# A router's tie count joined with its comparison, a choice made between two rankings, and the end of six tiles shared out over ScalarE and GpSimd

## The chip, the core and the metric

The kernel runs on one core of a Trainium2 chip. The metric is the device time of one execution in microseconds (us). Five engines work at once, each through its own queue in program order: TensorE (PE), VectorE (DVE), ScalarE (ACT), GpSimd (POOL) and SyncE (SP), which here only issues transfers. They wait for each other on counting semaphores.

## The reference, cut to what matters

All is float32. Two attention layers come first, then a mixture of experts, and at last a block that only the best three quarters of each batch's tokens go through:

```python
x = x + attention_2(attention_1(x, ...), ...)        # (2, 1024, 256)
h = moe(x)            # 8 experts, best 2 per token, plus one shared expert
x = x + ffn(h)

def moe(x):           # T = 2048 tokens
    scores = softmax((x @ wt.T + repeat(g @ wg.T)) / 2)
    w, idx = top_k(scores, 2);  w = w / (w.sum(-1) + 1e-20)
    y_e  = (leaky(x @ w_gate[e]) * (x @ w_up[e])) @ w_down[e]
    p    = (leaky(x @ sw_gate) * (x @ sw_up)) @ sw_down
    return sum over the two chosen e of w * y_e, + p

def ffn(h):           # (B, L, D) = (2, 1024, 256)
    k = int(L * 0.75)                                # 768 of 1024 tokens of a batch
    scores = einsum('bld,d->bl', h, w_router)
    _, top_idx = top_k(scores, k)
    processed = gelu(h[b, top_idx] @ w_block)
    return h.at[b, top_idx].set(processed)           # the others stay as they are
```

A token's score is higher than another's, or equal and at a lower index: that is the order that `top_k` uses, so equal scores have to be counted apart.

## The kernel before

The change lies in the last stage, some 60 us of 386, and in its preparation. P is 128, N is 1024 tokens to a batch, B is 2, TB is 8 tiles of 128 tokens to a batch, NT is 16 tiles in all, and NC_ is 4 chunks c of TT = 4 tiles, so that batch 0 is chunks 0 and 1 and batch 1 is chunks 2 and 3. Everything is written out by hand, with one program for each engine, and every engine keeps to its order.

**Sum of the experts.** The routed experts' results lie in the DRAM array YS, two rows to a token. SyncE reads them by chunks into YR (line 2327, 1 MB each, two buffers). Chunks 2 and 3 are read when VectorE is through with chunks 0 and 1. VectorE adds both rows, weighted, to the shared expert's result in Y (line 2748): for each chunk four tiles with k = 0, then four with k = 1, counted in `s_y`.

**Scores.** For each chunk TensorE turns Y (`result_turned`, line 2534), ScalarE copies it to FT (line 2617, two copies), TensorE makes the scores (`scores`, line 2542), ScalarE copies them to SR (line 2619), and TensorE lays each token's own score in a column (`own_scores`, line 2549). The four chunks follow each other, with the turning of chunk c + 1 ahead of `own_scores(c)`.

**Products.** `through_block(c)` (line 2557) multiplies a chunk's four tiles by w_block, two PSUM buffers in turn, and ScalarE applies the gelu (line 2623) to GE. All 16 tiles come behind the scores of all chunks, on TensorE as on ScalarE: `through_block(0)`, `masks_counted(0)`, `through_block(1)` to `(3)`, `masks_counted(1)`.

**Ranking.** `compare(b)` on VectorE goes through the 8 tiles q of a batch. Line 2761 compares the scores of tiles q to 7 with the tile's own scores, writes the mask GT[q] in bf16 and sums it into cnt. Line 2764 then counts the equal scores of lower index within the tile, into the scratch eqj. `masks_counted(b)` on TensorE (line 2573) adds up the masks of the tiles before (28 small products), so that what is counted in one direction need not be compared in the other. `compare(1)` writes over the same GT, and so waits for `masks_counted(0)`. `choose(b)` (lines 2772 to 2776) makes the rank, and `sel`, which is 1 for a token that goes through the block.

**End.** GpSimd makes Z = X1 + Y (line 2392), then GE = GE - Y (line 2395), each for all 16 tiles. VectorE makes Z = Z + sel * GE for all 16 (`finish`, line 2782; the profile names Z as WGU, GE as X, and X1 as AI, whose memory they use). SyncE writes the four chunks out in order (line 2331, 512 KB each). The order on VectorE is:

```python
compare(0)
compare(1)
choose(0)
finish(0)
choose(1)
finish(1)
```

## Time and profile before

| | us |
|---|---|
| median of 3 runs | 388.48 |
| lowest and highest | 386.22, 388.92 |
| profiled execution, its own time | 387.94 |
| its span, first to last instruction | 386.2 |
| TensorE busy in the span | 306.6 (79%) |
| VectorE busy | 207.0 (54%) |
| GpSimd busy | 182.3 (47%) |
| ScalarE busy | 135.9 (35%) |
| mean granted TensorE clock | 0.900 |

The busy shares are averages over all stages. The last stage begins at 330.48 us, when SyncE issues the first read of YS, so the questions about it are answered by the chain of waits and the timeline from there on. In what follows a time of day such as 364.93 is counted from the start of the span. A merged line of the timeline, such as "x8", gives the start of its first instruction and the time to the end of its last.

### The profile page before, as it was taken

To read this page: it belongs to the slowest core of one execution; us is meant where nothing else is said; L and a number is where in the kernel's file an instruction comes from. 1 tells how busy PE (TensorE), PEld (TensorE's weight loads), DVE (VectorE), ACT (ScalarE), POOL (GpSimd) and SP (SyncE) were. 2 spreads that over 40 slices of the span, in tenths; PEclk is the share of its full clock that TensorE was granted. 3 is DMA by queue.
4 is the path that set the end of the run, shared out by engine and by line. 5 is a ranking of instruction groups with operands and counts; after the bars stand their busy time and mean duration, and the time that the engine had idled before them with its cause. 6 is when DMAs were issued, how large, how long until landed. Compare 5 with 4: busy or idle time off the path is not lost.

```text
span 386.2 us, 5777 instructions
## 1 busy us (share of the span) xinstructions
PE 306.6 (79%) x1625; PEld 209.6 (54%) x1625; DVE 207.0 (54%) x730; ACT 135.9 (35%) x428; POOL 182.3 (47%) x306
## 2 busy tenths in 40 slices
PE   0499999988998978977692999719999997068990
PEld 0246767655774735443531665418888885035680
DVE  0724555521742237796458344504555553199996
ACT  1146676753111166572210000003555554014440
POOL 1308998863020000167404878732666666166380
PEclk9999999999999685798896799968999999558996
DMA  4779950000019800000100222243555441642006
GB/s 129 218 188 276 309 151 3 2 0 1 2 48 299 186 0 0 3 0 0 29 1 35 88 98 82 92 125 98 161 158 165 146 126 43 207 133 98 0 2 218
DMA packets 36186, 37.84 MB, mean 98 GB/s; under 512 B 5423, under 2 KB 31792, under 8 KB 36147
## 3 DMA queue, kind: packets, MB, share of 16 engines
q1 hardware_dynamic: 31762, 28.90, 26.5%
q0 software_dynamic: 3408, 8.41, 6.2%
q8 instruction: 17, 0.28, 0.3%
q10 hardware_dynamic: 976, 0.08, 0.2%
q14 instruction: 23, 0.18, 0.2%
HBM read 21.74 MB, written 16.55 MB: 99 GB/s over the span
## 4 chain that ended last, share of the span: by engine, by line
PE 22%; POOL 11%; DVE 9%; DMA 5%; issue 4%; ACT 1%; DVEq 0%; POOLq 0%; SPq 0%
PE psU L2489 9%; POOL XS L2369 4%; PE psY L2507 4%; POOL XS L2378 4%; DVE Y L2748 3%; DMA YR<-YS 3%; PE psG L2479 2%; POOL pause L2358 2%; DVE WGU L2782 2%; DVE GT L2761 2%; PE psY L2499 1%; PE psU L2557 1%; PE psG L2413 1%; PE psU L2413 1%; DVE eqj L2764 1%
## 5 line engine op out<-in xcount | busy, mean ns | idle before, releaser
L2386 POOL DMA_INDIRECT YS<-YB,IB x39 | 38.4, 984 | 36.3 <-issue 23.6
L2489 PE MATMUL psU<-WGU,XT 128*128 x156 | 42.1, 394 | 0.1
L2599 ACT COPY XT<-psG 128x256 f32<-128x256 f32 x39 | 14.7, 377 | 64.5 <-PE psG L2479 64.5
L1195 POOL TENSOR_SCALAR UU<-UU,rs 128x257 f32<-128x257 f32 x32 | 29.8, 931 | 0.0
L2489 PEld LDWEIGHTS psU<-WGU,XT 128*128 128x128 f32 x156 | 27.7, 198 | 2.8 <-issue 0.5
L1360 ACT ACTIVATE UU<-UU,nm 128x129 f32<-128x129 f32 x64 | 28.4, 453 | 0.7 <-DVE nm L1469 0.7
L1469 DVE CUSTOM_DVE_ANT_0 UU<-psS,BI 128x129 f32<-128x129 f32 x64 | 19.1, 356 | 17.2 <-PE psS L1248 17.2
L1194 POOL TENSOR_SCALAR UU<-UU,rs 128x129 f32<-128x129 f32 x32 | 19.6, 612 | 16.6 <-DVE rs L1479 16.4
L2369 POOL DMA_INDIRECT XS<-AI,SI x16 | 15.7, 981 | 23.1 <-DVE SI L2688 18.9
L2732 DVE TENSOR_SCALAR LK<-psU 128x128 f32<-128x128 f32 x39 | 11.4, 292 | 26.6 <-PE psU L2489 26.1
L2748 DVE SCALAR_TENSOR_TENSOR Y<-YR,W,Y 128x256 f32<-128x256 f32 x32 | 18.2, 640 | 12.5 <-DMA YR<-YS 12.5
L857 POOL TENSOR_TENSOR T<-Vn,wn 128x128 f32<-128x128 f32 x8 | 3.0, 401 | 46.4 <-DVE wn L953 46.3
L2424 PE MATMUL psY<-SD,HH 128*128 128x256 f32 x64 | 17.1, 415 | 7.9 <-DVE HH L2714 7.9
L2507 PE MATMUL psY<-WD,HT 128*128 x78 | 23.3, 382 | 0.0
L2479 PE MATMUL psG<-ident,XB 128*128 128x128 f32 x78 | 15.5, 285 | 9.4 <-DMA XB<-XS 9.4
L2424 PEld LDWEIGHTS psY<-SD,HH 128*128 128x128 f32 x64 | 13.1, 207 | 12.8 <-issue 10.3
L2392 POOL TENSOR_TENSOR WGU<-AI,Y 128x256 f32<-128x256 f32 x16 | 13.0, 840 | 14.4 <-DVE Y L2748 14.4
L1487 DVE COPY PT<-psTt 128x384 f32<-128x384 f32 x16 | 8.9, 555 | 20.3 <-PE psTt L1319 20.3
L930 DVE CUSTOM_DVE_ANT_0 UU<-psS,RA,NL 128x256 f32<-128x256 f32 x32 | 13.7, 480 | 10.4 <-ACT RA L797 9.6
L2479 PEld LDWEIGHTS psG<-ident,XB 128*128 128x128 f32 x78 | 11.4, 148 | 13.8 <-issue 10.2
L2606 ACT COPY HT<-psY 128x128 f32<-128x128 f32 x39 | 10.3, 265 | 22.3 <-PE psY L2499 21.7
L2534 PE MATMUL psG<-ident,Y 128*128 128x128 f32 x32 | 6.0, 349 | 14.9 <-DVE Y L2748 14.9
(313 smaller groups left out, 740.8 us busy)
## 6 DMA issues: line engine op xcount, KB each, us to landing
XS<-PZ SPq DMA_DIRECT2D x1, 5011.5 KB, 21.2
XB<-XS SPq DMA_DIRECT2D x39, 128.5 KB
YR<-YS SPq DMA_DIRECT2D x4, 1024.0 KB, 5.5
BI<-in_bias SPq DMA_DIRECT2D x4, 512.0 KB, 8.8
out_dram<-WGU SPq DMA_DIRECT2D x4, 512.0 KB, 3.0
X<-in_x SPq DMA_DIRECT2D x2, 768.0 KB, 9.8
BI<-in_bias SPq DMA_DIRECT2D x4, 256.0 KB, 8.0
Wo<-in_wo SPq DMA_DIRECT2D x1, 1024.0 KB, 6.9
```

The costliest lines, as they stand in the source:

```text
L1194: pool.tensor_scalar(U[:, he, 0:W1], U[:, he, 0:W1], rs[:, d, 2 * he:2 * he + 1], None, ALU.mult)
L1195: pool.tensor_scalar(U[:, he, W1:WU], U[:, he, W1:WU], rs[:, d, 2 * he + 1:2 * he + 2], None, ALU.mult).then_inc(n_done, 1)
L1360: act.activation(U[:, he, cols], U[:, he, cols], ACT.Exp, scale=-1.0, bias=nm[:, d, n:n + 1], accum_out=rs[:, d, n:n + 1]).then_inc(exp_do ...
L1469: dve.tensor_tensor_reduce(out=U[:, he, cols], in0=psS[2 * (d % 2) + he][:, cols], in1=BI[:, h, cols], scale=-1.0, scalar=-NEG, op0=ALU.ad ...
L2369: pool.indirect_dma_start(XS[:, :], bass.IndirectOffsetOnAxis(ap=SI[:, 0, t:t + 1], axis=0), AI[:, t, :], None).then_inc(s_g0[t // TB], 16)
L2378: pool.indirect_dma_start(XS[:, :], bass.IndirectOffsetOnAxis(ap=SI[:, 1, t:t + 1], axis=0), AI[:, t, :], None).then_inc(s_g1, 16)
L2386: pool.indirect_dma_start(YS[:, :], bass.IndirectOffsetOnAxis(ap=IB[:, b, n:n + 1], axis=0), YB[i][:, n, :], None, bounds_check=2 * NTOK - ...
L2424: mm = pe.matmul(psY[c % 2][:, t, :], HH[n % 2][:, t * P:(t + 1) * P], SD[:, m, :], start=m == 0 and t % 2 == 0, stop=m == NS_ - 1, skip_g ...
L2479: mm = pe.transpose(psG[b % 2][:, (k * SUB + n) * P:(k * SUB + n + 1) * P], XB[b % RING][:, n, k * P:(k + 1) * P], ident[:, :])
L2489: mm = pe.matmul(psU[b % 2][:, n * D:(n + 1) * D], XT[b % 2][:, k, n * P:(n + 1) * P], WGU[:, k, bass.ds(which[b], 1), :].rearrange("p a m ...
L2507: mm = pe.matmul(result(b)[:, n * D:(n + 1) * D], HT[b % 2][:, n * P:(n + 1) * P], WD[:, bass.ds(which[b], 1), :].rearrange("p a d -> p (a ...
L2748: dve.scalar_tensor_tensor(out=Y[:, t, :], in0=YR[c % 2][:, t % TT, k, :], scalar=W2[:, k, t:t + 1], in1=Y[:, t, :], op0=ALU.mult, op1=ALU ...
```

## The change

- In `compare`, the whole-row comparison starts one tile later and is left out for q = 7. The tile on the diagonal is compared by the other instruction, which takes `is_gt` in place of `is_equal`, multiplies by `upper` in place of `low`, and writes the first 128 columns of GT[q]. eqj is gone. TensorE now adds the diagonal masks too: 36 small products in place of 28.
- The sums that this leaves over are put into `need`, before the shared expert, with one reduction and one subtraction more on VectorE.
- `choose(0)` moves from behind `compare(1)` to within it, ahead of its first mask.
- `through_block(0)` moves from behind the scores of all chunks to behind `own_scores(1)`, and its four gelus move to behind chunk 1's copy to SR on ScalarE.
- Tiles 2 to 7 are ended without VectorE: ScalarE multiplies GE by `sel` (a copy with a scale, placed behind the gelu of tile u + 8) and GpSimd adds it to Z (placed behind the subtraction of tile u + 8). VectorE ends tiles 0, 1 and 8 to 15.
- The first read of YS becomes two, of two tiles each. VectorE starts on the first two tiles at the first of them.
- The chunks are written out in the order 0, 2, 1, 3. Chunks 0 and 1 wait for GpSimd's count as well as VectorE's.

```diff
@@ -2211,9 +2211,9 @@
                 low = tensor(st, "low", [P, P])
                 one_b = tensor(st, "one_b", [P, 1], BF16)
                 GT = [[tensor(st, f"GT{i}{q}", [P, (TB - q) * P], BF16) for q in range(TB)] for i in range(1)][0]
-                eqj = tensor(st, "eqj", [P, 4, P])
                 cnt = tensor(st, "cnt", [P, NT, 2])
                 need = tensor(st, "need", [P, TB])
+                ahead = tensor(st, "ahead", [P, 1])
                 rank = tensor(st, "rank", [P, NT])
                 sel = tensor(st, "sel", [P, NT])
                 GE = X
@@ -2232,7 +2232,7 @@
                 s_pe = sem(st, "s_pe")
                 PE_GUIDED, PE_LOGITS, PE_TURNED, PE_TOTAL, PE_PLACES = 1, 2, 3, 4, 5
                 s_route = sem(st, "s_route")
-                GUIDES, READ, SHIFTED, MARKED, TOTALS, SLOTTED, SLOT_IDS, EXPERT_IDS = range(1, 9)
+                GUIDES, READ, SHIFTED, MARKED, TOTALS, SLOTTED, SLOT_IDS, EXPERT_IDS, CHOSEN = range(1, 10)
                 s_ex = sem(st, "s_ex")
                 s_g0 = [sem(st, f"s_g0{g}") for g in range(2)]
                 s_i1 = sem(st, "s_i1")
@@ -2270,6 +2270,11 @@
                 blk = st.enter_context(nc.Block())
 
                 SPACED = 2 * NT - 1
+                DIFFERENT = SPACED + NT + TB
+                BY_DVE = 2
+                ENDED = [0]
+                for u in range(TB):
+                    ENDED.append(ENDED[-1] + (2 if u >= BY_DVE else 1))
 
                 def bank(c, k):
 
@@ -2321,13 +2326,18 @@
                     for i in range(RING):
                         sp.wait_ge(s_ys[i], 16 * SUB * len(range(i, NBK, RING)))
                     picks = YS.rearrange("(t p k) d -> p t k d", p=P, k=2)
+                    sp.dma_start(YR[0][:, 0:2, :, :], picks[:, 0:2, :, :]).then_inc(s_xb[0], 16)
                     for c in range(NC_):
                         if c >= 2:
                             sp.wait_ge(s_y, 2 * TT * (c - 1))
-                        sp.dma_start(YR[c % 2][:, :, :, :], picks[:, TT * c:TT * c + TT, :, :]).then_inc(s_yr[c % 2], 16)
+                        lo = 0 if c else 2
+                        sp.dma_start(YR[c % 2][:, lo:TT, :, :], picks[:, TT * c + lo:TT * c + TT, :, :]
+                                     ).then_inc(s_yr[c % 2], 16)
                     ov = out.rearrange("b (t p) d -> p (b t) d", p=P)
-                    for c in range(NC_):
-                        sp.wait_ge(s_z, TT * c + TT)
+                    for c in (0, 2, 1, 3):
+                        if c < 2:
+                            sp.wait_ge(pool_done, DIFFERENT + ENDED[TT * c + TT])
+                        sp.wait_ge(s_z, (BY_DVE, BY_DVE, BY_DVE + TT, BY_DVE + 2 * TT)[c])
                         sp.dma_start(ov[:, TT * c:TT * c + TT, :], Z[:, TT * c:TT * c + TT, :]).then_inc(s_out, 16)
                     sp.wait_ge(s_out, 16 * NC_)
 
@@ -2390,9 +2400,18 @@
                     for t in range(NT):
                         pool.wait_ge(s_y, 2 * TT * (t // TT) + TT + t % TT + 1)
                         pool.tensor_tensor(Z[:, t, :], X1[:, t, :], Y[:, t, :], ALU.add).then_inc(pool_done, 1)
-                    for t in range(NT):
+                    for t in range(TB):
                         pool.wait_ge(s_ge, t + 1)
                         pool.tensor_tensor(GE[:, t, :], GE[:, t, :], Y[:, t, :], ALU.subtract).then_inc(pool_done, 1)
+                    pool.wait_ge(pool_done, DIFFERENT)
+                    pool.wait_ge(s_route, CHOSEN)
+                    for t in range(TB, NT):
+                        pool.wait_ge(s_ge, t + 1)
+                        pool.tensor_tensor(GE[:, t, :], GE[:, t, :], Y[:, t, :], ALU.subtract).then_inc(pool_done, 1)
+                        u = t - TB
+                        if u >= BY_DVE:
+                            pool.wait_ge(s_ex, 2 + u - BY_DVE)
+                            pool.tensor_tensor(Z[:, u, :], Z[:, u, :], GE[:, u, :], ALU.add).then_inc(pool_done, 1)
 
                 @blk.tensor
                 def _(pe):
@@ -2565,16 +2584,18 @@
                         if c + 1 < NC_:
                             result_turned(c + 1)
                         own_scores(c)
+                        if c == 1:
+                            through_block(0)
+
                     def masks_counted(b):
-                        for q in range(1, TB):
+                        for q in range(TB):
                             t = b * TB + q
-                            pe.wait_ge(s_gt, t)
-                            for a in range(q):
+                            pe.wait_ge(s_gt, t + 1)
+                            for a in range(q + 1):
                                 mm = pe.matmul(larger(t), GT[a][:, (q - a) * P:(q - a + 1) * P], one_b[:, :],
-                                               start=a == 0, stop=a == q - 1)
+                                               start=a == 0, stop=a == q)
                             mm.then_inc(s_cs, 1)
 
-                    through_block(0)
                     masks_counted(0)
                     for c in range(1, NC_):
                         through_block(c)
@@ -2618,9 +2639,14 @@
                         act.wait_ge(s_sc, c + 1)
                         act.copy(SR[:, :, :].rearrange("p b n -> p (b n)")[:, c * CH:(c + 1) * CH], scored(c)
                                  ).then_inc(s_sr, 1)
-                    for t in range(NT):
-                        act.wait_ge(s_h, t + 1)
-                        act.activation(GE[:, t, :], psU[t % 2][:, 0:D], ACT.Gelu_apprx_tanh).then_inc(s_ge, 1)
+                        for t in (range(TT) if c == 1 else range(TT, NT) if c == NC_ - 1 else ()):
+                            act.wait_ge(s_h, t + 1)
+                            act.activation(GE[:, t, :], psU[t % 2][:, 0:D], ACT.Gelu_apprx_tanh).then_inc(s_ge, 1)
+                            u = t - TB
+                            if u >= BY_DVE:
+                                act.wait_ge(s_route, CHOSEN)
+                                act.wait_ge(pool_done, DIFFERENT)
+                                act.activation(GE[:, u, :], GE[:, u, :], ACT.Copy, scale=sel[:, u:u + 1]).then_inc(s_ex, 1)
 
                 @blk.vector
                 def _(dve):
@@ -2701,7 +2727,10 @@
                     dve.wait_ge(s_wb, 32)
                     for k in range(KD):
                         dve.tensor_copy(wr_m[:, k, :], wr_c[:, k:k + 1].broadcast_to([P, P])).then_inc(s_wr, 1)
-                    chain(dve.tensor_scalar(need[:, :], exp_f[:, 0:TB], -float(P), float(TOPK), ALU.mult, ALU.add))
+                    dve.wait_ge(s_con, 10)
+                    chain(dve.tensor_reduce(ahead[:, :], low[:, :], AX_X, ALU.add), True)
+                    chain(dve.tensor_scalar(need[:, :], exp_f[:, 0:TB], -float(P), float(TOPK), ALU.mult, ALU.add), True)
+                    chain(dve.tensor_tensor(need[:, :], need[:, :], ahead[:, 0:1].broadcast_to([P, TB]), ALU.subtract), True)
                     chain(dve.memset(cnt[:, :, :], 0.0), True)
 
                     for n in range(NJ + 1):
@@ -2740,9 +2769,14 @@
                     dve.wait_ge(bh_done, NBK)
                     for c in range(NC_):
                         tiles = range(TT * c, TT * c + TT)
-                        dve.wait_ge(s_yr[c % 2], 16 * (c // 2 + 1))
+                        if c:
+                            dve.wait_ge(s_yr[c % 2], 16 * (c // 2 + 1))
+                        else:
+                            dve.wait_ge(s_xb[0], 16 * (len(range(0, NBK, RING)) + 1))
                         for k in range(2):
                             for t in tiles:
+                                if not c and not k and t == 2:
+                                    dve.wait_ge(s_yr[0], 16)
                                 if k:
                                     dve.wait_ge(s_y, 2 * TT * c + t % TT + 1)
                                 dve.scalar_tensor_tensor(out=Y[:, t, :], in0=YR[c % 2][:, t % TT, k, :], scalar=W2[:, k, t:t + 1],
@@ -2754,40 +2788,41 @@
                         ts = slice(b * TB, b * TB + TB)
                         chain(dve.tensor_copy(SC[:, ts], bank(3, b)[:, 0:TB]), True)
                         if b:
-                            dve.wait_ge(s_cs, b * (TB - 1))
+                            choose(0)
                         for q in range(TB):
                             t = b * TB + q
                             own = SC[:, t:t + 1]
-                            dve.tensor_scalar(GT[q][:, :], SR[:, b, q * P:N], own, 0.0, ALU.is_gt, ALU.add,
-                                              accum_out=cnt[:, t, 0:1]).then_inc(s_gt, 1)
-                            after(3)
-                            chain(dve.scalar_tensor_tensor(out=eqj[:, count[0] % 4, :], in0=SR[:, b, q * P:(q + 1) * P],
-                                                           scalar=own, in1=low[:, :], op0=ALU.is_equal, op1=ALU.mult,
-                                                           accum_out=cnt[:, t, 1:2]))
+                            if q + 1 < TB:
+                                chain(dve.tensor_scalar(GT[q][:, P:], SR[:, b, (q + 1) * P:N], own, 0.0, ALU.is_gt, ALU.add,
+                                                        accum_out=cnt[:, t, 0:1]))
+                            dve.scalar_tensor_tensor(out=GT[q][:, 0:P], in0=SR[:, b, q * P:(q + 1) * P], scalar=own,
+                                                     in1=upper[:, :], op0=ALU.is_gt, op1=ALU.mult,
+                                                     accum_out=cnt[:, t, 1:2]).then_inc(s_gt, 1)
 
                     def choose(b):
                         ts = slice(b * TB, b * TB + TB)
                         dve.wait_ge(s_gt, TB * (b + 1))
                         after()
                         chain(dve.tensor_reduce(rank[:, ts], cnt[:, ts, :], AX_X, ALU.add), True)
-                        dve.wait_ge(s_cs, (b + 1) * (TB - 1))
-                        chain(dve.tensor_tensor(rank[:, b * TB + 1:b * TB + TB], rank[:, b * TB + 1:b * TB + TB],
-                                                psG[b][:, 1:TB], ALU.subtract), True)
-                        chain(dve.tensor_tensor(sel[:, ts], rank[:, ts], need[:, :], ALU.is_lt), True)
-
-                    def finish(b):
-                        dve.wait_ge(pool_done, SPACED + b * TB + TB)
-                        for t in range(b * TB, b * TB + TB):
-                            dve.wait_ge(pool_done, SPACED + NT + t + 1)
-                            dve.scalar_tensor_tensor(out=Z[:, t, :], in0=GE[:, t, :], scalar=sel[:, t:t + 1],
-                                                     in1=Z[:, t, :], op0=ALU.mult, op1=ALU.add).then_inc(s_z, 1)
+                        dve.wait_ge(s_cs, (b + 1) * TB)
+                        chain(dve.tensor_tensor(rank[:, b * TB:b * TB + TB], rank[:, b * TB:b * TB + TB],
+                                                psG[b][:, 0:TB], ALU.subtract), True)
+                        dve.tensor_tensor(sel[:, ts], rank[:, ts], need[:, :], ALU.is_lt).then_inc(s_route, 1)
+                        dve.wait_ge(s_route, CHOSEN + b)
+
+                    def finish(t):
+                        dve.scalar_tensor_tensor(out=Z[:, t, :], in0=GE[:, t, :], scalar=sel[:, t:t + 1],
+                                                 in1=Z[:, t, :], op0=ALU.mult, op1=ALU.add).then_inc(s_z, 1)
 
                     compare(0)
                     compare(1)
-                    choose(0)
-                    finish(0)
+                    dve.wait_ge(pool_done, DIFFERENT)
+                    for t in range(BY_DVE):
+                        finish(t)
                     choose(1)
-                    finish(1)
+                    for t in range(TB, NT):
+                        dve.wait_ge(pool_done, DIFFERENT + ENDED[t - TB] + 1)
+                        finish(t)
 
 
 
```

## Rows read from the trace of the kernel before

**Rows 1.** Page, its first line.
```profile
span 386.2 us, 5777 instructions
```
**Rows 2.** Chain that ended last, in order of time, last stage: start us, us, what.
```profile
330.48 5.52 DMA YR<-YS
...
345.54 5.39 DMA YR<-YS
...
360.48 3.65 PE psU L2557 x16
```
**Rows 3.** Timeline, ScalarE and TensorE: start us, us, engine, line, op, idle before.
```profile
352.08 1.08 ACT L2617 COPY FT<-psG 128x512 f32<-128x512 f32 x2
352.36 0.40 PE L2549 MATMUL psY<-ident,SR 1*128 1x1 f32 x4
353.21 1.98 PE L2542 MATMUL psY<-FT,wr_m 128*128 128x512 f32 x4 [0.45 <-ACT FT L2617]
355.60 1.09 PE L2534 MATMUL psG<-ident,Y 128*128 128x128 f32 x8 [0.40 <-DVE Y L2748]
...
359.44 0.58 ACT L2619 COPY SR<-psY 128x512 f32<-128x512 f32 x1 [2.07 <-PE psY L2542]
360.04 1.28 ACT L2623 ACT_TABLE_LOAD   x1
...
361.58 0.38 ACT L2623 ACTIVATE X<-psU 128x256 f32<-128x256 f32 x1 [0.26 <-PE psU L2557]
...
364.17 0.38 ACT L2623 ACTIVATE X<-psU 128x256 f32<-128x256 f32 x1 [0.48 <-PE psU L2557]
...
364.67 10.61 PE L2557 MATMUL psU<-WB,FT 128*128 128x256 f32 x48
...
375.12 0.84 PE L2573 MATMUL psG<-one_b,GT 128*128 128x1 bf16 x28
```
**Rows 4.** Timeline, VectorE: two steps of compare(0), then compare(1) begins.
```profile
355.65 1.28 DVE L2761 TENSOR_SCALAR_CACHE_REDUCE GT<-SR,SC 128x1024 bf16<-128x1024 f32 x1
...
356.86 0.35 DVE L2764 SCALAR_TENSOR_TENSOR eqj<-SR,SC,low 128x128 f32<-128x128 f32 x1
...
357.13 1.14 DVE L2761 TENSOR_SCALAR_CACHE_REDUCE GT<-SR,SC 128x896 bf16<-128x896 f32 x1
...
364.93 1.28 DVE L2761 TENSOR_SCALAR_CACHE_REDUCE GT<-SR,SC 128x1024 bf16<-128x1024 f32 x1 [0.21 <-PE psG L2573]
```
**Rows 5.** Timeline, the end: choice, last eight of finish, and the four writes.
```profile
374.38 0.16 DVE L2774 TENSOR_TENSOR rank<-rank,psG 128x7 f32<-128x7 f32 x1
...
374.83 4.20 DVE L2782 SCALAR_TENSOR_TENSOR WGU<-X,sel,WGU 128x256 f32<-128x256 f32 x8
...
377.48 5.73 SPq L2331 DMA_DIRECT2D out_dram<-WGU  x4
...
379.55 3.26 DVE L2782 SCALAR_TENSOR_TENSOR WGU<-X,sel,WGU 128x256 f32<-128x256 f32 x8
...
381.25 0.37 SPq L2331 DMA_DIRECT2D out_dram<-WGU  x1
```
**Rows 6.** Timelines, GpSimd beside VectorE, then GpSimd alone.
```profile
339.46 2.46 POOL L2392 TENSOR_TENSOR WGU<-AI,Y 128x256 f32<-128x256 f32 x3
...
339.70 1.72 DVE L2748 SCALAR_TENSOR_TENSOR Y<-YR,W,Y 128x256 f32<-128x256 f32 x2
...
177.73 2.10 POOL L871 TENSOR_TENSOR AI<-X,CB 128x256 f32<-128x256 f32 x3
```
**Rows 7.** Windows, after TensorE's last work: busy by engine, clock, DMA share, GB/s.
```profile
380.20:380.40 0.20, 0.00 (x0) 0.00 (x0) 0.20 (x2) 0.00 (x0) 0.00 (x0) 0.83 1.00 343
```
**Rows 8.** Groups by line: TensorE's wait ahead of the routed experts, then ScalarE's forms.
```profile
L2479 PE MATMUL psG<-ident,XB 128*128 128x128 f32 x78 | 15.5, 285 | 9.4 <-DMA XB<-XS 9.4
...
L813 ACT ACTIVATE UU<-UU,nm 128x256 f32<-128x256 f32 x32 | 15.8, 499 | 0.0
L2623 ACT ACT_TABLE_LOAD x1 | 1.3, 1283 | 0.0
```

## Prediction

> **What bounds the kernel now.** I read the chain of waits first. From 330.48 us on it tells of one serial stretch: the read of YS, the sums over chunks 0 and 1, from 345.54 the read of chunk 3, and VectorE's last sums, until its comparisons begin at 355.65 [rows 2, 4]. The busy shares would have said TensorE, but in this stage the bound changes hands, so I went through the timeline piece by piece.
>
> First, TensorE and ScalarE carry chunks 2 and 3 to the scores, and both wait for each other: products 1.98, copy 0.58, and so on [rows 3]. `own_scores(3)` ends about 360.48, `through_block(0)` takes 3.65 more [rows 2], and `masks_counted(0)` follows. Second, VectorE starts compare(0) at 355.65 and compare(1) at 364.93 [rows 4], and is never idle for long until the end. TensorE has by then 12 tiles of products to do, from 364.67 for 10.61 us, and `masks_counted(1)` ends at 375.96 (375.12 + 0.84) [rows 3]. So the two run nearly level, TensorE to 375.96 and VectorE's comparisons to about 374.1. Third, VectorE alone does the sixteen steps of finish, from 374.83 to 382.81 (379.55 + 3.26) [rows 5]. The last write is issued at 382.84 (377.48 + 5.73, less the 0.37 of one issue), and the span ends at 386.2 [rows 1, 5]: 3.35 us behind a single last write.
>
> **The reads of YS.** VectorE starts on half of chunk 0 at the first transfer. The second half still has to come, and by the chain the whole 1 MB lands 5.52 us after its issue [rows 2]. So only the two steps that can be done ahead are won. One step takes 0.40 us: (3.26 - 0.48)/7 in the last finish, of the same form [rows 5]. That is 0.8 us at most. The second issue costs SyncE 0.37 of it at worst, so I take 0.6, between 0.4 and 0.8. Chunks 2 and 3 wait in the same chain and move up with it. VectorE's comparisons then begin at 355.05, and `own_scores(1)` ends at 352.16 (352.36 + 0.40 - 0.6) [rows 3].
>
> **Through_block(0) moved up.** It costs TensorE 3.65 us again, 352.16 to 355.81. But ScalarE keeps its order, and FT of chunk 2 now stands behind four gelus. The load of the gelu's table, 1.28 us, starts when the copy to SR is done, about 351.5, and ends about 352.8; the first gelu comes 1.10 after the start of the products (360.48 to 361.58), so at 353.3, and the load is hidden [rows 2, 3]. The fourth gelu ended 0.42 after the four tiles' products (364.17 + 0.38 against 360.48 + 3.65), so now at 356.23. Then come two copies to FT, 1.08 [rows 3], so `scores(2)` starts at 357.38; before it started at 353.21. From there on nothing waits for VectorE any more. The steps are: scores 1.98, turning and the two copies behind the copy to SR 1.77, scores 2.0, copy and wait 0.66, own scores 0.41. Sum 6.8: `own_scores(3)` ends at 364.2. Before, the same point came at 360.48, but with 3.65 of products still to do, that is at 364.13. **So what is moved up gains nothing.** The 0.41 us for which TensorE waited for VectorE's sums, and 0.6 of the reads, are paid out again for gelus and copies that once lay beside products and now hold TensorE up for 1.57 us.
>
> How the load's own cost is counted matters here. The trace has 1.28 us of load at 360.04 and the gelu at 361.58, which waited for TensorE by the profile, so at most 0.26 lie behind the load [rows 3]. The Trainium skill (ScalarE: Activation LUTs, What ACT_TABLE_LOAD costs) puts a drain of about 1.38 us beside each load. If it lay behind the load, an estimate from that page would hold chunk 2 back by some 0.5 us more. The row doesn't show it, and the measurement decides.
>
> **Masks and choice.** 36 small products for 28: at 0.84/28 each that is 0.24 more on TensorE, so it ends `masks_counted(0)` at about 365.1. compare(0) lasted at most 9.1 us (355.65 to 364.93, less the wait) and lasts 1.2 less now (below), so it is done at 363 at the latest, and VectorE stands idle for 2 us or more, where before it never waited over 0.21 [rows 4]. It can't go on, because GT is in use, and SR of batch 1 is only there at 363.7. choose(0)'s two last steps, 0.45 (374.38 to 374.83 [rows 5]), now stand ahead of compare(1), which starts at 365.65, against 364.93.
>
> **Compare.** The first step, of 1024 columns, took 1.21 us of VectorE (355.65 to 356.86), and the step on the diagonal 0.27 (356.86 to 357.13) [rows 4]. Each whole-row step becomes one tile shorter and the longest falls away, while the diagonal ones stay: 1.2 us less per batch. The new form of the diagonal step (another comparison, a bf16 result) is in no row. It is nearest to the old one of the same shape, so I take 0.27; it can't come below the 0.13 by which one tile more or less changes a whole-row step (1.28 - 1.14), and at the whole-row step's full price of 0.34 or so it would add 0.5 in a batch. compare(1) lasted 9.2 us (364.93 to about 374.1, just ahead of the choice [rows 4, 5]), so now 8.0: it ends at 373.6, 0.5 earlier. That is all that remains of 2.4 us saved.
>
> **What TensorE still has to do.** 12 tiles from 365.1. In the trace the way from 364.67 to the end of the masks took 11.3 us [rows 3]; with 8 more masks 11.5, so 376.6. VectorE fills the time with finish of tiles 0 and 1, and then waits. sel of batch 1 is there at 377.1, against 379.5 before [rows 5]. The eight last steps of finish would need 3.26 us alone [rows 5], and end at 380.4, 2.4 earlier than now.
>
> **ScalarE's share.** For tiles 10 to 15 a gelu of 0.38 and a copy with a scale stand behind each other. No row has that copy. The lower bound is the gelu's 0.38, the upper 0.50, the exponential from and to SBUF of the same shape [rows 8]. With waits that is 0.8 to 0.93, against 0.863 of one tile on TensorE ((364.17 - 361.58)/3) [rows 3]. I take 0.86, level with TensorE; the upper bound would add 0.4 in six tiles.
>
> **GpSimd's share.** It gets six additions more, and its second eight subtractions wait for choose(0) and for gelu 8, which ends about 370.1. Fourteen steps then follow. Alone, one takes 0.69 us ((2.10 - 0.72)/2). Beside VectorE's steps of two inputs it is different: both go in step, one each in 0.86 (two of VectorE's in 1.72, three of GpSimd's in 2.46), though VectorE alone needs 0.40 [rows 5, 6]. VectorE is at such steps for part of the time, so I take the mean of both: GpSimd ends at 370.1 + 14 x 0.78 = 381.1, and by the bounds 379.8 (0.69) to 382.1 (0.86). VectorE meanwhile makes its four first steps of batch 1 at 0.86, not 0.40. Tiles 8 to 11 are done at 377.15 + 4 x 0.86 = 380.6, tile 15 at about 382.5, against 382.8 before. The saving on VectorE is lost by the contention.
>
> By the Trainium skill (SBUF - State Buffer, SBUF: two separate sides) one of the two engines holds the shared ports for a whole instruction and the other fully blocks. Taken so, a pair would take 0.40 + 0.69 = 1.09, and that is a rival below. The row has 0.86.
>
> **The writes.** A write of 512 KB occupies the queues for 1.53 us at 343 GB/s [rows 7], and the last, alone, needs 3.35 from its issue to the end (above). Chunk 2 is issued at 380.65. Chunk 1 waits for GpSimd's last step, 381.1, and chunk 3 for 382.5. Before, they were spread out. Now three stand within 1.9 us and share the same queues: 380.65 + 3.35 + 2 x 1.53 = 387.1 for the end.
>
> **The sum.** 387.1 against 386.2 of span [rows 1]: 0.9 us longer. What lies around the span, 1.7 us, stays, so 387.94 becomes 388.8. The median of the runs is 0.5 above the profiled execution and they differ by 2.7 among themselves, so I say 388.9. The small work that is added ahead of the shared expert (a reduction, a subtraction, a wait for constants) costs nothing: the shared expert is done so early that TensorE then waits 9.4 us for the routed experts' first transfer [rows 8]. Without that cover it would be some 0.5, at the price of the choice's steps.
>
> **Rivals.** *The forecast: the moved products gain nothing, contention and piled-up writes take the rest*, 387.8 to 389.8, 0.60.
> *The ends don't collide.* If VectorE went on at 0.40 beside GpSimd at 0.69, chunk 2 would be issued at 378.8, chunk 1 at 380.4 and chunk 3 at 380.8: span 385.4, 387.1 in all. The rows of lockstep speak against it, but there GpSimd partly waited for VectorE's result, so it isn't excluded: 0.20.
> *The whole instruction blocks.* At 1.09 per pair tile 11 is done at 381.5, 0.9 later, and the writes with it; with the sums' own delays 389.7 to 390.6. 0.08.
> *ScalarE or TensorE goes slow: the side of over 1% slower.* Each change between gelu and scaled copy could reload the table: 1.28 x 2 for six tiles, 15 us, over 400. It decides from two loads per tile. Against it: one load of 1.28 in the stage, at the first gelu [rows 3], and none for the copies behind an exponential. Or TensorE's clock falls to 1.2 GHz during its new idle time. In the trace it fell at about 380.3, 4.3 us after its last work [rows 3, 7]; the new gaps are 1.6. If it fell, 12 tiles would take 10 us more: 399. Together, and with dearer diagonal steps, 0.07.
> *Faster by over 1%.* The products would have to hide wholly, as if ScalarE could take FT of chunk 2 first: 3.65 less on TensorE, of which compare(0)'s end near 363 lets 2 to 3 through. Even then the span is 384, 2 to 3 less than before, so this needs another gain: 0.05.
>
> **How the numbers follow.** The predicted time is that of the first case. From 386.2 (the second, with 0.9 for the scatter of the runs) to 390.8 (the third) about nine in ten are held with the uncertainty of a median of few runs, so I give 386.2 to 390.8. One per cent is 3.9 us, about what a measurement can tell from no change. Faster by over 1%: 0.05. Slower: 0.07. Within: 0.88.
>
> **What would show it.** `scores(2)` at about 357.4, behind gelu 3 on ScalarE. VectorE idle from about 363 to 365.2, ended by `masks_counted(0)`. compare(1) 1.2 us shorter. `masks_counted(1)` at about 376.6. Steps of finish at 0.86 while GpSimd works. The last three writes within 2 us of each other. The forecast is wrong if ScalarE's copies to FT of chunk 2 don't wait for gelus, if finish goes at 0.40, or if more than one table is loaded in the stage.

## Result, and the profile after

| | before | after |
|---|---|---|
| median, us | 388.43 (20 runs) | 390.74 (20 runs) |
| lowest and highest | 385.38, 392.27 | 387.50, 394.48 |
| ratio after/before, 95% interval | | 1.0069, 1.0043 to 1.0095 |
| profiled execution | 387.94 | 387.5 |
| its span | 386.2 | 385.4 |
| outside its span | 1.74 | 2.10 |

The time moved by 0.7%, so the kernel stayed within 1%, a little slower. The ratios leave out executions over 1.5% above the fastest of their kernel, and by medians the step is 2.3 us (0.6%). The medians mislead a little: ten runs of after lie at 387.5 to 389.6 and ten at 391.9 to 394.5, so that its median falls between two levels, where no run is, while of before 13 lie at 385.4 to 388.9 and seven at 390.9 to 392.3. The means of all twenty are 388.8 and 390.6, 1.8 us apart. The trace says something else: its span is 0.8 us shorter. Two further comparisons (below) gave 0.9988 (0.9950 to 1.0026) and 1.0035 (0.9997 to 1.0073). Most of what follows is about why one trace, one ratio and a sum can disagree by a few us.

The chain of waits of after, last stage (start us, us, what), answers [rows 2]:

```profile
330.90 4.64 DMA YR<-YS
335.54 0.02 issue
335.57 3.40 DVE Y L2782 x6
...
350.24 3.67 PE psU L2576 x16
353.93 0.39 ACT X L2644
354.31 0.97 ACT FT L2638 x2
...
355.33 2.00 PE psY L2561 x4
...
362.03 0.98 PE psG L2595 x36
363.01 10.47 PE psU L2576 x48
373.48 0.89 PE psG L2595 x36
...
375.18 3.50 DVE WGU L2814 x4
```

VectorE's long comparison is gone from the chain; TensorE and ScalarE carry it from 339.11 on. The moved products stand in it at 350.24, and behind them the fourth gelu and the copies to FT of chunk 2, which once lay beside other work.

The timeline of after (start us, us, engine, line, operation, idle before) answers [rows 3] and [rows 5]:

```profile
334.33 0.88 DVE L2782 SCALAR_TENSOR_TENSOR Y<-YR,W,Y 128x256 f32<-128x256 f32 x2 [9.53 <-DMA YR<-YS]
335.57 8.26 DVE L2782 SCALAR_TENSOR_TENSOR Y<-YR,W,Y 128x256 f32<-128x256 f32 x14 [0.35 <-DMA YR<-YS]
...
349.67 1.28 ACT L2644 ACT_TABLE_LOAD   x1
351.33 0.38 ACT L2644 ACTIVATE X<-psU 128x256 f32<-128x256 f32 x1 [0.38 <-PE psU L2576]
...
355.33 1.98 PE L2561 MATMUL psY<-FT,wr_m 128*128 128x512 f32 x4 [1.44 <-ACT FT L2638]
...
362.88 10.61 PE L2576 MATMUL psU<-WB,FT 128*128 128x256 f32 x48
363.12 0.16 DVE L2808 TENSOR_TENSOR rank<-rank,psG 128x8 f32<-128x8 f32 x1 [0.59 <-PE psG L2595]
...
373.93 7.22 SPq L2341 DMA_DIRECT2D out_dram<-WGU  x4
375.18 5.56 DVE L2814 SCALAR_TENSOR_TENSOR WGU<-X,sel,WGU 128x256 f32<-128x256 f32 x8
378.37 0.91 POOL L2414 TENSOR_TENSOR WGU<-WGU,X 128x256 f32<-128x256 f32 x1
```

The last eight steps of finish take 5.56 us, where they took 3.26 [rows 5]: GpSimd works beside the first four, which take 3.50. The last write is issued at 380.78 (373.93 + 7.22 - 0.37), 2.1 earlier than before, but the span ends 4.6 us behind it, not 3.35.

### The profile page after: what moved, and what is told of

Its sections match the earlier page's. It is cut to its first block, busy times and chain, and to the rows that moved or that the text cites. A ratio compares the mean times of both kernels' runs of the same rounds, so it can differ in the third digit from the quotient of the medians.

```text
span 385.4 us, 5821 instructions
## 1 busy us (share of the span) xinstructions
PE 306.7 (80%) x1641; PEld 210.6 (55%) x1641; DVE 205.4 (53%) x722; ACT 138.0 (36%) x434; POOL 186.8 (48%) x312
## 4 chain that ended last, share of the span: by engine, by line
PE 28%; POOL 11%; issue 4%; DVE 3%; DMA 3%; ACT 2%; DVEq 0%; SPq 0%; POOLq 0%
PE psU L2508 9%; POOL XS L2379 4%; PE psY L2526 4%; POOL XS L2388 4%; PE psU L2576 4%; PE psY L2561 3%; PE psG L2498 2%; POOL pause L2368 2%; DVE WGU L2814 1%; DMA YR<-YS 1%; PE psY L2518 1%; ACT FT L2638 1%; PE psG L2432 1%; PE psU L2432 1%; DVE Y L2782 1%
## 5 line engine op out<-in xcount | busy, mean ns | idle before, releaser
L2508 PE MATMUL psU<-WGU,XT 128*128 x156 | 41.3, 389 | 0.1
L2379 POOL DMA_INDIRECT XS<-AI,SI x16 | 15.7, 981 | 24.5 <-DVE SI L2714 20.4
L2388 POOL DMA_INDIRECT XS<-AI,SI x16 | 15.5, 970 | 4.4 <-issue 2.5
```

Of the source, the lines that this page charges most:

```text
L2379: pool.indirect_dma_start(XS[:, :], bass.IndirectOffsetOnAxis(ap=SI[:, 0, t:t + 1], axis=0), AI[:, t, :], None).then_inc(s_g0[t // TB], 16)
L2388: pool.indirect_dma_start(XS[:, :], bass.IndirectOffsetOnAxis(ap=SI[:, 1, t:t + 1], axis=0), AI[:, t, :], None).then_inc(s_g1, 16)
L2508: mm = pe.matmul(psU[b % 2][:, n * D:(n + 1) * D], XT[b % 2][:, k, n * P:(n + 1) * P], WGU[:, k, bass.ds(which[b], 1), :].rearrange("p a m ...
```

## Experiments

Every trace is measured by its last stage, from the first issue of a read of YS to the end of the span, because the start of that stage differs between executions of one and the same kernel. "Total" adds what lies outside the span. "48 products" is the time of the products behind `masks_counted(0)`; its normal value is 10.61. The last three kernels have 40 products there, so the column is empty. Each row is one trace, so a few tenths of a us between two rows can be chance.

| kernel | stage starts | stage | outside | total | 48 products |
|---|---|---|---|---|---|
| before | 330.48 | 55.7 | 1.74 | 57.5 | 10.61 |
| before_again | 329.42 | 55.5 | 1.71 | 57.2 | 10.61 |
| after | 330.48 | 54.9 | 2.10 | 57.0 | 10.61 |
| after_look3 | 332.07 | 55.0 | 2.11 | 57.1 | 10.61 |
| after_third | 335.19 | 55.5 | 2.06 | 57.6 | 10.61 |
| after_again | 329.44 | 57.1 | 2.10 | 59.2 | 12.29 |
| after_look2 | 336.01 | 57.1 | 2.05 | 59.1 | 12.29 |
| e_order | 335.59 | 55.9 | 2.05 | 58.0 | 10.61 |
| e_unmove | 330.63 | 55.3 | 2.11 | 57.4 | 10.61 |
| e_unsplit | 329.14 | 56.2 | 2.13 | 58.3 | 10.61 |
| e_unshare | 335.53 | 54.0 | 1.75 | 55.7 | 10.61 |
| b_split | 334.24 | 54.0 | 1.69 | 55.6 | 10.61 |
| no_move_no_share | 331.36 | 53.6 | 1.74 | 55.4 | 10.61 |
| filled | 331.72 | 55.1 | 2.06 | 57.1 | 10.61 |
| filled2 | 335.19 | 55.5 | 2.11 | 57.6 | 10.61 |
| longer | 329.54 | 59.6 | 2.11 | 61.7 | 12.29 |
| longer2 | 331.54 | 59.5 | 2.17 | 61.6 | 12.29 |
| best5 | 334.19 | 53.0 | 1.98 | 55.0 | |
| best8 | 335.06 | 52.5 | 1.69 | 54.2 | |
| best8_again | 332.26 | 52.3 | 1.76 | 54.1 | |

### The kernel before against itself

No edit.

> The kernel before, unchanged, timed against itself to see how its executions differ. Its 20 runs spread from 385.4 to 392.3 us, and its one trace has 387.94 us, so it is not among its fastest. If the kernel has several levels that hang on when TensorE's granted clock rises in the last stage (at 349.3 us in its trace, at 345.1 us in the changed kernel's), this run's trace shows the rise at another time or a span near 383.6 us for a run near 385.4. If the levels have nothing to do with that rise, the span will move while the rise stays near 349. Ratio 1.000.

Ratio 0.9959 (0.9914 to 1.0004) for the same kernel. Its trace has the clock rise at 345.5 and not at 349.5, and the stage is hardly shorter, 55.5 for 55.7: `scores(2)` starts 0.97 us earlier, counted from the start of the stage, but then TensorE waits 1.11 us for VectorE's sums, where it waited 0.40 [rows 3]. (Below, "early" and "late" mean this rise: late when the turning of chunk 1 still runs partly at 1.2 GHz and takes 1.46 to 1.92 us in place of 1.04 to 1.09. Early are before_again, after, after_look3, filled, e_unmove and e_unsplit; all others are late, and before is the latest of them. In the changed kernel the late rise costs 0.5 us of stage: 55.5 in after_third and filled2, 54.9 to 55.1 in after, after_look3 and filled.)

```profile
351.18 1.98 PE L2542 MATMUL psY<-FT,wr_m 128*128 128x512 f32 x4 [0.39 <-ACT FT L2617]
354.27 1.09 PE L2534 MATMUL psG<-ident,Y 128*128 128x128 f32 x8 [1.11 <-DVE Y L2748]
```

So that rise is not what sets the levels of the runs' times. A larger difference lies 180 us earlier. The traces differ in TensorE's granted clock at 150 to 170 us: ten of the twenty have 0.77 to 0.81 there and begin the last stage at 329.1 to 332.1, the other ten have 0.59 and begin it at 331.5 to 336.0. The window of before, then that of b_split (busy us and instructions of PE, PEld, DVE, ACT, POOL, then clock, DMA share, GB/s):

```profile
150.00:170.00 20.00, 18.74 (x110) 10.21 (x109) 15.29 (x53) 11.52 (x41) 4.70 (x8) 0.79 0.01 2
```
```profile
150.00:170.00 20.00, 19.31 (x86) 9.75 (x84) 11.52 (x39) 9.38 (x32) 4.62 (x8) 0.59 0.01 2
```

110 products in 20 us against 86. In 88 executions of before with a recorded clock (one of 773 us left out), 58 have a mean clock of 0.8975 or more and average 387.4 us, and 30 have less and average 391.3. The first instruction that the change adds runs at 209.6 us in after, so this stretch has nothing of the change in it. Why the clock differs there stays open.

### The read split in two, alone

```diff
 # before, with:
+                    sp.dma_start(YR[0][:, 0:2, :, :], picks[:, 0:2, :, :]).then_inc(s_xb[0], 16)
+                        lo = 0 if c else 2
 # ... and VectorE's two waits as in after
```

> The kernel before with only the first read of YS split in two. By the traces VectorE's sums of chunk 0 ended 1.6 us earlier in the changed kernel, where I had reckoned with 0.6. If that is the split's doing and passes on, the time is 0.996 to 0.997 of before. If the part of it that came from TensorE's clock rising 4 us earlier is not the split's, 0.998.

0.9952 (0.9917 to 0.9986), and a stage of 54.0, against 55.7 in before, whose rise is later still, and 55.5 in before_again, whose rise is early: 1.5 to 1.8 us, two to three times my 0.6. VectorE's sixteen sums, before and then in b_split, end 15.0 and 13.3 us behind the first issue (330.48 and 334.24):

```profile
336.46 9.06 DVE Y L2748 x16
```
```profile
338.41 9.12 DVE L2756 SCALAR_TENSOR_TENSOR Y<-YR,W,Y 128x256 f32<-128x256 f32 x16 [9.80 <-DMA YR<-YS]
```

The chain of waits of after (above) shows how. The second half landed at 335.54, 4.64 us behind its issue, half a microsecond ahead of the whole read (336.0 [rows 2]). VectorE also went on 0.02 us later, where it had waited 0.41 more for the first step of a stretch (336.05 to 336.46). That makes 0.9, and the two steps done ahead add 0.8.

### The products put back

```diff
 # after, with:
-                        if c == 1:
-                            through_block(0)
+                    through_block(0)
                     masks_counted(0)
 # ... and on ScalarE the four gelus with them
```

> The changed kernel with through_block(0) and its four gelus put back behind the scores of all chunks. My theory, that the move gains nothing and costs nothing: same as the changed kernel within 0.5 us, about 1.006 of before. Rival, that the move itself loses: TensorE no longer waits 1.4 us for the copies to FT of chunk 2, scores(2) starts near 351 instead of 355.3 us, and the time falls to before or below, 0.997 to 1.000.

0.9989 (0.9949 to 1.0029), stage 55.3 against 54.9 and 55.0 of after with the same early rise of the clock. The move is worth 0.2 to 0.4 us of TensorE's 3.65, so near nothing, as forecast. The ratio alone doesn't decide: I had expected 1.006, and 0.9989 lies where the rival had it, but the changed kernel itself came to 0.9988 in its second comparison. The rival is refuted on the stage: `scores(2)` did start at 350.85, but TensorE then waited for the sums and nothing came of it.

```profile
354.12 1.09 PE L2553 MATMUL psG<-ident,Y 128*128 128x128 f32 x8 [1.29 <-DVE Y L2780]
```

### Nothing shared

```diff
 # after, with:
-                BY_DVE = 2
+                BY_DVE = TB
-                    for c in (0, 2, 1, 3):
+                    for c in range(NC_):
 # ... and the wait for s_z as in before
```

> The changed kernel with all sixteen tiles ended by VectorE again, and the four writes in their old order. If contention and piled-up writes at the end are what costs, the last write stands alone again (3.35 us from issue to end, not 4.6), but VectorE has 6 more steps of 0.4 to 0.86 us before choice 1, for which it has only about 1 us of idle time: about 1.003 of before. If the sharing does pay, this is slower than the changed kernel, 1.010 or more.

0.9929 (0.9897 to 0.9962), total 55.7 against 57.0 to 57.6 of after. Its rise is late, so after_third is its neighbour: sharing the end of six tiles costs 1.9 us. Of these, 1.3 are behind the last issue of a write (4.66 and 3.36), 0.31 outside the span, and 0.24 ahead of that issue: VectorE ends no later with all sixteen tiles to do. Its last eight steps in after_third, then in e_unshare:

```profile
380.45 5.56 DVE L2814 SCALAR_TENSOR_TENSOR WGU<-X,sel,WGU 128x256 f32<-128x256 f32 x8
```
```profile
382.85 3.26 DVE L2814 SCALAR_TENSOR_TENSOR WGU<-X,sel,WGU 128x256 f32<-128x256 f32 x8
```

Counted from the start of the stage they begin 2.1 us earlier with the share (45.26 and 47.32) and take 2.3 longer. So of the two theories, the one of contention and piled-up writes holds for where the time goes, with one part, outside the span, that it doesn't explain. Its forecast of 1.003 missed: without the share the kernel is faster than before.

### The changed kernel again

No edit.

> The changed kernel, unchanged, beside the kernel before on another chip. From the first read of YS to the end of the span it took 54.9 us in its trace against 55.7 and 55.5 in two of before, and 0.36 us more outside the span, so by the traces of the last stage it should be 0.3 us faster, while its 20 runs were 1.007 of before. If that ratio belongs to the kernel, it comes again, 1.005 or more, and the stage of reads starts later than in before. If it came from the levels between which the earlier stages jump, the ratio is 0.998 to 1.002 here.

Ratio 0.9988. And a trace with 57.1 us of stage, 2.1 more than the first one. The rise is late here, so its neighbour is after_third (55.5), and 1.6 us are left to explain. The windows of after, then of after_again, columns as above (the first of each pair differ in length and only show the clock at full speed):

```profile
358.00:361.50 3.50, 2.51 (x10) 1.00 (x8) 3.45 (x20) 1.43 (x3) 0.00 (x0) 1.00 0.00 0
363.00:366.00 3.00, 3.00 (x16) 2.64 (x16) 2.81 (x7) 1.02 (x3) 1.38 (x2) 1.00 0.00 0
```
```profile
358.00:361.00 3.00, 2.04 (x5) 0.68 (x4) 2.41 (x16) 0.93 (x2) 0.00 (x0) 1.00 0.00 0
363.00:366.00 3.00, 3.00 (x9) 2.37 (x8) 2.96 (x10) 0.38 (x1) 0.72 (x1) 0.50 0.00 0
```

At 362.6 the granted clock falls from 2.4 to 1.2 GHz, for some 3.5 us, though TensorE is busy. 9 products against 16 are done in these 3 us, and the 48 products take 1.7 us longer, which makes the whole tail late:

```profile
362.41 12.29 PE L2576 MATMUL psU<-WB,FT 128*128 128x256 f32 x48
```

### The order of the writes

```diff
-                    for c in (0, 2, 1, 3):
+                    for c in (0, 1, 2, 3):
```

> The changed kernel with the writes in order 0, 1, 2, 3 (chunk 1 still waits for GpSimd). If the pile of three writes is what lengthens the end, this changes nothing, since chunk 1 becomes ready 0.6 us after chunk 2: last issue to end of span 4.6 us again. If the order is to blame for the 0.36 us more outside the span (2.11 against 1.74), these go back to 1.74; if the sharing is, they stay.

4.84 us from the last issue to the end, 2.05 outside: the order is to blame for neither. The stage of 55.9 stands beside 55.5 of after_third (both late), so the new order may be worth 0.4. One trace only.

### The read whole again

The edit takes the split out of after, and VectorE's second wait with it.

> The changed kernel with the first read of YS whole again. The split kernel b_split took 54.0 us for the stage against 55.6, so the split would be worth 1.6 and the rest of the change would cost: this takes 56.3 to 56.6 us for the stage. If the late chain hides the split, 55 us.

56.2 against 54.9 and 55.0, all with the early rise: the split is worth 1.1 to 1.2 in the changed kernel too, most of what it is worth alone.

### Ties and choice

```diff
 # the edits of e_unmove and e_unshare together
```

> The changed kernel with its products back in their old place and nothing shared: only the split read, the joined ties and the choice between the rankings are left. b_split, the split alone, took 54.0 us for the stage, and e_unshare, which has the move as well, 54.0. If ties and choice are worth nothing as long as TensorE's products set when batch 1 can be chosen, this takes 53.8 to 54.2. If they are worth the 1 us and more that they take off VectorE, 52.5 to 53.

53.6, between the two cases, and nearer to the first. The joined ties and the choice between the rankings bring 0.2 to 0.3 us over b_split (totals 55.4 and 55.6), of the 2.4 us that I had reckoned they take off VectorE. And e_unshare, which differs from this kernel by the move alone, has 55.7: without the share the move costs 0.3 us, where with the share it brought 0.2 to 0.4. Single traces don't settle its sign; its size is near nothing in both.

### Does the clock fall again, and why

> The changed kernel once more, for its trace. In one of two traces TensorE's granted clock was at half for some 4 us at 362 to 366 us and its 48 products took 12.29 us in place of 10.61. If such a fall belongs to the changed kernel, because TensorE now waits more between 350 and 362 us, it comes again in one of the two looks here and the stage takes about 57 us; if it was chance, both have 10.61 us and 55 to 56 us.

> As after_look2: a further trace of the changed kernel, to see how often the clock falls between 355 and 370 us. 48 products in 10.61 us without a fall, 12.3 with one.

12.29 in one of the two. With after, after_again and after_third it is two of five traces of the changed kernel. To tell whether the gap of 1.44 us ahead of `scores(2)` matters, I filled it and lengthened it:

```diff
 # filled, behind the moved products on TensorE
+                            for _ in range(10):
+                                pe.transpose(bank(3, 1)[:, 2 * P:3 * P], ident[:, :], ident[:, :])
```

> The changed kernel with ten turnings of the identity (128x128, into PSUM columns that nobody reads) behind the moved products, so that TensorE's 1.44 us of waiting for the copies to FT of chunk 2 is filled. If the gap brings the fall of the clock, the 48 products take 10.61 us in both runs of this. If it does not, 12.29 in about one of two.

> As filled, a second execution: 10.61 us for the 48 products if the gap matters, and a stage of 55.0 us.

```diff
 # longer, behind the fourth gelu on ScalarE
+                                for spare in (XT[0][:, 0, :], XT[0][:, 1, :], XT[1][:, 0, :], XT[1][:, 1, :], HT[0][:, :]):
+                                    act.copy(spare, HT[1][:, :])
```

> The changed kernel with five copies of 128x128 more on ScalarE behind the fourth gelu, so that TensorE waits some 2.5 us for chunk 2 in place of 1.44. If the gap brings the fall of the clock, the fall comes in both runs of this, and earlier or longer than before. If not, in about one of two as before; all later work is 1.1 us later in both cases.

> As longer, a second execution: 12.29 us or more for the 48 products if the gap matters.

TensorE's scores of chunk 2, in filled and then in longer:

```profile
356.68 1.98 PE L2561 MATMUL psY<-FT,wr_m 128*128 128x512 f32 x4 [0.35 <-ACT FT L2640]
```
```profile
355.87 3.61 PE L2561 MATMUL psY<-FT,wr_m 128*128 128x512 f32 x4 [2.43 <-ACT FT L2638]
```

Filled (0.35 us of the gap are left): no fall in either. Lengthened (2.43 us): it falls in both, and twice in each. The windows of longer, columns as above:

```profile
353.00:356.00 3.00, 0.57 (x4) 0.17 (x2) 3.00 (x9) 2.34 (x9) 3.00 (x6) 0.96 0.00 0
356.00:359.00 3.00, 3.00 (x4) 1.28 (x5) 3.00 (x13) 0.00 (x0) 0.55 (x1) 0.50 0.00 0
366.00:369.00 3.00, 3.00 (x9) 2.34 (x8) 3.00 (x7) 0.77 (x2) 1.35 (x2) 0.50 0.00 0
```

The copies lengthen the gap by 1.0 us and the stage grows by 4.0 against after_third (59.5 for 55.5, all late). With the products in their old place (before, before_again, b_split, e_unmove, no_move_no_share) there was no fall in five traces, and in the other kernels with the gap (e_order, e_unsplit, e_unshare) none in three. So the fall came in both traces with the longer gap, in two of eight with the gap as it is, and in none of ten without it: the five above, filled and filled2, and the three of best5 and best8 (below). That points at the gap, and only the longer one is clear. For the gap as it is the groups are small, and two traces of the ten speak against it: before_again and e_unmove have gaps of 1.11 and 1.29 us in the same stretch, where TensorE waits for VectorE's sums, and as much idle time in sum, and no fall. Filling it was tried twice, and two traces without a fall could be chance. So what brings the fall in the changed kernel stays open.

### The changed kernel a third time

No edit.

> The changed kernel a third time. The stage takes 54.9 to 55.0 us without the fall of the clock and 57.1 with it, plus 0.36 outside the span, against 55.6 of before: 0.3 us faster or 1.9 slower. With the fall in a third to a half of the executions the mean is 0.4 to 0.8 slower: 1.001 to 1.004. If the first comparison told of something else that costs 2.7 us, 1.006 or more.

1.0035 (0.9997 to 1.0073), as expected for a fall in some executions, and a stage of 55.5 without a fall, 0.5 above the expected 55.0 (the rise is late). By level of the mean clock, all 46 executions of after average 388.0 (26 runs) and 392.6 (20 runs), against 387.4 and 391.3 of before: 0.6 and 1.3 us slower. The totals give 57.0 to 57.6 without the fall, level with before, and 59.1 and 59.2 with it, 1.8 slower. The mean of the five totals is 58.0, 0.7 above before. The first 20 executions had ten at the low level, where before had seven of 20, and 30 of the 88. Three runs more at a level that lies over 4 us higher are 0.7 of the 1.8 us between the means of the first comparison; the other 1.1 lie within the levels, and a fall now and then fits them. Whether the change makes the low level more frequent, the runs don't settle (20 of 46 against 37 of 108).

### A version that beats both

```diff
 # after, with BY_DVE = 5 (best5) or TB (best8), writes in order 0 to 3, and
+                            through((0, 1))          # behind own_scores(1)
+                            through((2, 3))          # ahead of own_scores(3)
+                    through((4, 5))                  # ahead of masks_counted(0)
+                        for t in (range(2) if c == 2 else ()):   # ScalarE: gelus 0 and 1
+                            act.wait_ge(s_h, t + 1)              # between FT and SR of chunk 2
 # ... the other tiles follow in order, on TensorE and on ScalarE
```

> The changed kernel with other places for the moved products and a smaller share: tiles 0 and 1 of the products behind own_scores(1), with their gelus between chunk 2's copies to FT and its copy to SR, where ScalarE waits for scores anyway; tiles 2 and 3 ahead of own_scores(3); tiles 4 and 5 ahead of masks_counted(0); GpSimd and ScalarE end only tiles 5 to 7, and the chunks are written in order 0 to 3. My theory, that the move fails because ScalarE's queue holds up chunk 2 and the share because three writes pile up: scores(2) starts about 22 us after the first read of YS, the writes are spread, the stage takes 51.3 to 53 us against 55.6, and the time is 0.990 to 0.994 of before. Rival, that VectorE's work is all that counts: 53.5 to 54.5 us, like b_split.

> best5 with no tile shared: VectorE ends all sixteen. best5 took 53.0 us from the first read of YS to the end of the span and 1.93 us outside it. If the sharing of late tiles is worth what GpSimd takes off VectorE, this takes 54.0 us or more for the stage and 1.74 outside. If the good places of the products alone made the gain, 53.0 to 53.4 and 1.74, and the time is 0.993 of before.

> best8 again, with more runs, on the same chip as the changed kernel. Its stage took 52.5 us (335.06 to 387.6) against 55.6 of before, with nothing more outside the span: 3.1 us less, 0.992. Rival: its first ratio of 0.9947 is right and the stage's gain is partly lost elsewhere.

best5: 0.9950 (0.9907 to 0.9993), with a stage of 53.0, at the upper end of what I had expected. best8: 0.9947 (0.9902 to 0.9991), and 0.9898 (0.9847 to 0.9948) the second time, with stages of 52.5 and 52.3, lower than either of my two cases. Totals of 54.1 and 54.2 against 57.2 and 57.5: 3.1 us less, or 0.992, which lies between the two ratios. `scores(2)` of best8 stands directly behind the products, with the gelus no longer ahead of the copies:

```profile
354.26 0.87 PE psG L2553 x8
355.13 0.34 PE psY L2568 x4
355.47 1.92 PE psU L2576 x8
357.39 1.73 PE psY L2561 x4
```

Leaving the sharing out gives 0.8 more (totals of best5 and best8), so my theory that a small share pays was wrong.

## Why the prediction was right and where it failed

**What held.** The time stayed within 1%. ScalarE's queue ate the move: `scores(2)` was forecast 5.2 us behind the end of `own_scores(1)` (352.16, 357.38), and came 5.1 behind it (350.24, 355.33). VectorE stood idle ahead of compare(1), though for 1.2 us in two waits (0.62 for `own_scores(3)`, 0.59 for `masks_counted(0)`) and not for 2. compare(1) took 8.5 us (363.52 to 372.04), for which 8.0 were forecast and 9.2 measured before: the joined ties saved 0.7 and not 1.2. TensorE's last masks set the start of finish for batch 1, so the half microsecond did no harm. Finish went in step with GpSimd, 0.87 per tile for four tiles (3.50). The last issue stood 4.62 from the end; forecast were 4.6 (387.1 - 382.5).

The whole instruction doesn't block. GpSimd's and VectorE's instructions of two inputs take turns in 0.87 each, in the first four steps of finish for batch 1, for which all that they need was ready, where 0.40 + 0.69 = 1.09 was the price of the rival. The Trainium skill (SBUF - State Buffer, SBUF: two separate sides) has one lock for the whole instruction; the 0.87 is less than the 1.09 that this would make, so by these rows the two overlap in part. The load of the gelu's table took 1.28 and the gelu came 0.38 behind it, again waiting for TensorE. The Trainium skill (ScalarE: Activation LUTs, What ACT_TABLE_LOAD costs) counts a drain of about 1.38 us beside the load; at most these 0.38 can lie behind it here. And the scaled copies cost 0.499 us each, the upper bound exactly, without holding TensorE up; no table was loaded for them:

```profile
L2649 ACT ACTIVATE X<-X,sel 128x256 f32<-128x256 f32 x6 | 3.0, 499 | 0.0
L2644 ACT ACT_TABLE_LOAD x1 | 1.3, 1283 | 0.0
```

**The reads: a term mis-sized.** Forecast 0.6 won, at most 0.8. Measured 1.5 to 1.8 alone, and 1.1 to 1.2 in the changed kernel. I took the landing of the whole as that of the second half, and the 0.41 us from landing to first step as fixed. Both moved. The span of the first trace is 385.4 and not 387.1, and all of that is there early: `own_scores(1)` ended at 350.24, where 352.16 was forecast. Some 1.3 of the 1.9 are there in after_third too, whose rise of the clock is late; the other 0.6 came with the early rise, which is luck.

**The fall of the clock: the step that failed.** The sum has no term for a fall of TensorE's clock. The rival set 4.3 us of idle time, after which the clock had fallen behind the last work of before [rows 3, 7], against gaps of 1.6, and it reckoned with 10 us of loss; so the chance was put into 0.07 and the cost into no number. In its place, the clock fell in two of five traces of the changed kernel, with no gap longer than 1.44 us since its rise, for some 3.5 us, and cost 1.6 us of stage (57.1 for 55.5 of after_third). A small loss with a fair chance was ruled out by a large one with none. One row on an engine that stops for good says little on one that stops for short times again and again.

**Outside the span: the second step that failed.** "What lies around the span, 1.7 us, stays" was wrong: 1.74 became 2.10, 0.36 us in every execution. It follows the number of shared tiles: 1.69 to 1.76 with none (seven traces), 1.98 with three (best5), 2.05 to 2.17 with six (twelve traces); over the 88 executions of before it is 1.76 on average, over the 46 of after 2.11. What it is stays open; e_order only shows that the order of the writes isn't it.

**The sum.** The totals lead from before to after in single steps: 57.2 and 57.5 (before), 55.6 with the split (b_split), 55.4 with ties and choice (no_move_no_share), 55.7 with the move (e_unshare), 57.6 with the share and the new order of writes (after_third). So the split takes 1.5 to 1.8 off, the share puts 1.9 on, and the rest is 0.3 and less. Before and after without a fall are level (57.2 and 57.5; 57.0 to 57.6). With a fall it is 1.8 more. I had forecast +0.9 for every execution. The mean over all recorded executions is 1.3 us higher (388.7 of 88, 390.0 of 46), which is near the forecast by luck: it is made of nothing in some executions and nearly 2 us in others, and of more executions at the slow level of the earlier stage. That last part, and so the exact size of the ratio 1.0069, stays open.

**The range.** 390.74 lies in the range of 386.2 to 390.8, at its edge. The range allowed for scatter at its lower end only. It was held by luck too, since the median of after fell between two groups of runs, the higher of which begins at 391.9.

## What to carry to other kernels

Before work is moved into an idle place of one engine, look at the in-order queue of the engine that takes its result: here four gelus stood ahead of the copies that the next step needed, and the products of six tiles in three smaller pieces, with the gelus behind those copies, gave 1.5 us (e_unshare 55.7, best8 54.2). Price a share for another engine with what both engines do to each other, and with the transfers that then become ready together; 0.40 us steps became 0.87, and three writes came out within 2.1 us (378.71 to 380.78). And where executions of one kernel differ by more than the change, measure the changed stage in several traces from its own start, not the span of one.

## What the runs showed of the hardware

TensorE's granted clock can fall to half while the engine has work: in two of eight traces it fell 17 us after it had risen to 2.4 GHz, with gaps of 0.34 to 1.44 us in between, and rose again some 3.5 us later. With the longest gap at 2.43 us it fell in both traces, twice each. From execution to execution the granted clock also differs in a stage that the change doesn't touch (0.77 to 0.81 against 0.59 at 150 to 170 us), and executions of before with a low mean clock take about 4 us more. GpSimd's and VectorE's instructions of two inputs, 0.69 and 0.40 us alone, went in turns of 0.87. The second 0.5 MB of a read landed 4.64 us behind its own issue and 5.06 behind the first, while the whole 1 MB took 5.52. And a wait in the middle of VectorE's steps cost 0.02 us behind the landing, where the first step of a stretch came 0.41 behind.
